# Opening pass of a transformer tower: three-part bf16 split by subtraction on TensorE, and another closing point for one of VectorE's loops

## The reference

```
h = W.T[x]                                        # embedding rows, (16, 512, 128)
x1 = layernorm(h)
left, right = x1 @ W1, W2 @ x1.T                  # W1 is 128x10, W2 is 10x128
h = h + softmax(left @ right / sqrt(512)) @ x1
x2 = layernorm(h)
h = h + ffn(x2)    # router picks 1 of 4 spatial and 1 of 4 temporal experts for each batch;
                   # three attentions of 8 heads (spatial S, temporal T and causal, cross C); an MLP
```

## Time and profile before

| | |
|---|---|
| three runs | 1670.5, 1671.6, 1672.09 us; median 1671.6 us |
| the profiled execution | 1672.9 us, span of its trace 1671.1 us |
| mean granted TensorE clock | 0.942 |
| TensorE, VectorE, ScalarE, GpSimd busy | 91%, 75%, 66%, 61% of the span |
| opening pass (start to `logits(0)`) | 0 to 134.8 us |
| second half of `embed_and_mix` | to about 250 us |
| `attend` | about 250 to 1555 us |
| `feed_forward` | to 1671.1 us |

### The profile page before, as it was taken

One profiled execution on the slowest core, in us unless ns is written; L12 is line 12 of the kernel. 1 busy time (PEld: TensorE's weight loads), 2 busy tenths in 40 slices (PEclk: granted clock), 3 DMA queues, 4 the chain that ended last, 5 costly groups with the idle time before them and its releaser, 6 DMA issues. The chain is left out here.

```text
span 1671.1 us, 37358 instructions
## 1 busy us (share of the span) xinstructions
PE 1517.6 (91%) x8662; PEld 661.0 (40%) x8662; DVE 1245.2 (75%) x3454; ACT 1106.5 (66%) x2137; POOL 1020.2 (61%) x1375
## 2 busy tenths in 40 slices
PE   3657976889999999999999999999999999875998
PEld 1215962233333333333333334333333333212665
DVE  6885866578887988888798888879788888353442
ACT  3333760647878788787877878787787878823333
POOL 6841435466686777767677777767767775523443
PEclk9867976889999999999999999999999999957999
DMA  1321118355554565456456546545655654121221
GB/s 48 77 52 30 45 32 110 49 77 74 75 84 66 72 78 83 64 77 82 64 75 78 79 63 80 79 63 79 78 76 62 86 70 50 15 25 33 64 63 57
DMA packets 134645, 109.27 MB, mean 65 GB/s; under 512 B 24128, under 2 KB 127552, under 8 KB 134592
## 3 DMA queue, kind: packets, MB, share of 16 engines
q1 hardware_dynamic: 132544, 104.45, 42.8%
q0 software_dynamic: 2048, 4.20, 1.0%
HBM read 19.26 MB, written 8.39 MB: 17 GB/s over the span
## 5 line engine op out<-in xcount | busy, mean ns | idle before, releaser
L1122 ACT ACTIVATE probs<-psum 128x512 f32<-128x512 f32 (+3 forms) x1536 | 755.7, 548 | 226.4 <-PE psum L1237 215.6
L1022 DVE TENSOR_REDUCE mx_S<-psum 128x1 f32<-128x512 f32 x512 | 326.3, 681 | 47.9 <-PE psum L1217 47.3
L1022 DVE TENSOR_REDUCE mx_C<-psum 128x1 f32<-128x512 f32 x512 | 318.0, 677 | 45.2 <-PE psum L1217 45.2
L1018 DVE CUSTOM_DVE_ANT_0 psum<-psum,causal 128x128 f32<-128x128 f32 (+3 forms) x512 | 243.3, 509 | 98.0 <-PE psum L1217 95.4
L1217 PE MATMUL psum<-ks_S,qs_S 96*128 96x512 bf16 x512 | 196.8, 395 | 10.8 <-DMA ks_S<-parts_k 6.1
L1217 PE MATMUL psum<-ks_C,qs_C 96*128 96x512 bf16 x512 | 199.7, 398 | 4.5 <-DMA ks_C<-parts_k 1.3
L1237 PE MATMUL psum<-qs_C,ks_C 99*128 99x512 bf16 x512 | 189.3, 385 | 3.6 <-ACT probs L1122 3.2
L1237 PE MATMUL psum<-qs_S,ks_S 99*128 99x512 bf16 x512 | 191.2, 385 | 0.2
L903 POOL CAST parts_q<-f_q 128x512 bf16<-128x512 f32 x48 | 29.3, 611 | 226.2 <-ACT f_q L1113 225.7
L1217 PE MATMUL psum<-ks_T,qs_T 96*128 96x128 bf16 (+3 forms) x512 | 156.1, 307 | 1.6 <-DVE mx_S L1022 1.0
L1237 PE MATMUL psum<-qs_T,ks_T 99*128 99x256 bf16 (+3 forms) x512 | 152.5, 302 | 2.8 <-ACT probs L1122 1.5
(11 more groups left out here) (182 smaller groups left out, 2720.2 us busy)
## 6 DMA issues: line engine op xcount, KB each, us to landing
qs_S<-parts_q SPq DMA_DIRECT2D x96, 128.0 KB, 4.4
ks_S<-parts_k SPq DMA_DIRECT2D x96, 128.0 KB, 4.8
qs_T<-parts_q SPq DMA_DIRECT2D x96, 128.0 KB, 4.4
ks_T<-parts_k SPq DMA_DIRECT2D x96, 128.0 KB, 4.6
qs_C<-parts_q SPq DMA_DIRECT2D x96, 128.0 KB, 4.3
ks_C<-parts_k SPq DMA_DIRECT2D x96, 128.0 KB, 5.0
w_in_S<-in_s_in SPq DMA_DIRECT2D x16, 257.0 KB, 2.8
w_in_T<-in_t_in SPq DMA_DIRECT2D x16, 257.0 KB, 2.7
```

The lines of the kernel that those rows point to most:

```text
L1018: nc.vector.tensor_tensor_reduce(tile[:, 0:last_key], tile[:, 0:last_key], causal[:, T - last_key:T], 1.0, NEG, ALU.add, ALU.max, mx[kind] ...
L1022: nc.vector.tensor_reduce(mx[kind][:, n:n + 1], tile, AX_X, ALU.max, negate=True).then_inc(reduced, 1)
L1122: nc.scalar.activation(probs[:, group_place(kind, b, n // 4), n % 4, t0:T], psum[:, LOGITS + ring_place(kind, b, n, RC), t0:T], ACT.Exp, s ...
```

## The change

Two things are changed.

**The opening pass.** `w12` is now 128 columns wide: the left weights stand six times beside each other (columns 10g to 10g+9), the right weights six times from column 64. One projection (fp32, 128 rows out) so gives the six copies of each factor at once, already stacked in PSUM. The remainders are then formed in the same PSUM bank: ScalarE casts the bank to bf16 (`part[0]`), TensorE adds `minus[:, 0] @ part[0]` to it (`take`), where `minus` is -1 on the diagonal of those groups that want a later part and 0 elsewhere; ScalarE casts again (`part[1]`), TensorE takes that away from the groups that want the third part. What is left in each group, rounded to bf16, is its part: ScalarE copies rows 0 to 63 to `qsd`, VectorE rows 64 to 127 to `ksd`. The score matmuls contract over 64 rows instead of 96. Gone are VectorE's subtraction, GpSimd's low part and the 12 stacking DMAs for a pair. The projection bank is doubled (banks 5 and 7).

ScalarE now normalises (four activations with scale and bias; VectorE makes `shift` = -mean * rstd), and SyncE copies `xs` to `X` by one DMA for each batch. Scores follow three batches late. GpSimd's gathers wait for the load of the ids alone. `logits(0)` waits for the last reduction instead of for `neg_step >= 6`; that wait is now ahead of `mix(0)`.

**VectorE's loop in `attend`** closes at slot 2, step 8: ahead of the ninth cross score.

```
-DVE_LOOP_AT = 1, 8
+DVE_LOOP_AT = 2, 8
...
-        MAXIMA, LR, TURN, POOLED = 4, 5, 6, 7
-        LO_LAG, SCORE_LAG, MAX_LAG = 4, 6, 7
+        MAXIMA, LR, TURN, POOLED = 4, (5, 7), 6, 7
+        TURN_LAG, PART_LAG, SCORE_LAG = 1, 2, 3
+        LATER = ((30, 60), (74, 94), (104, 114)), ((50, 60), (84, 94))
...
-                stack(0)
-                with sp.Fori(1, B // 2) as pair:
-                    stack(pair)
+                def keep(b, odd):
+                    sp.wait_ge(normed1, b + 1)
+                    sp.dma_start(X[:, bass.ds(NB * b, NB), 0:P], xs[:, odd, :, :]).then_inc(x_kept[odd], 16)
...
-                pool.wait_ge(loaded, 16 * LOADS)
+                pool.wait_ge(ids_in, 16)
...
-                for b in range(B + LO_LAG):
-                    if exists(b):
-                        fetch(b)
-                    if exists(b - LO_LAG):
-                        low_part(b - LO_LAG)
+                for b in range(B):
+                    fetch(b)
...
+                nc.vector.memset(minus[:], 0.0).then_inc(minus_set, 1)
                 dve.wait_ge(consts, 2)
+                dve.wait_ge(minus_set, 1)
+                for k, columns in enumerate(LATER):
+                    for a, e in columns:
+                        last = nc.vector.tensor_scalar(minus[:, k, a:e], ident[:, a:e], -1.0, None, ALU.mult)
+                last.then_inc(minus_set, 1)
+                nc.vector.memset(ksd[RA1:RA1 + 32, :, :], 1.0)
...
+                def take(c, odd, k):
+                    pe.wait_ge(part_ready[k], c + 1)
+                    nc.tensor.matmul(psum[:, LR[odd], :], minus[:, k, :], part[k][:], start=False, stop=(k == 1),
+                                     skip_group_check=True).then_inc(taken[k], 1)
...
-                pe.wait_ge(x_kept, B)
-                pe.wait_ge(neg_step, 6)
+                pe.wait_ge(x_kept[0], 8 * B)
+                pe.wait_ge(x_kept[1], 8 * B)
+                pe.wait_ge(reduced, 2 * B)
```

More of the change, by code:

```diff
@@ L269, in _ @@
                 sp.dma_start(norm_cols[:], norms).then_inc(loaded, 16)
[L271 to L280, removed]
-                stack(0)
-                with sp.Fori(1, B // 2) as pair:
-                    stack(pair)
+                def keep(b, odd):
+                    sp.wait_ge(normed1, b + 1)
+                    sp.dma_start(X[:, bass.ds(NB * b, NB), 0:P], xs[:, odd, :, :]).then_inc(x_kept[odd], 16)
+                halves_of_pairs(sp, keep, 1, B // 2, B // 2)
                 for half in range(2):
@@ new lines, in factors @@
+                    if exists(b):
+                        act.wait_ge(shift1, b + 1)
+                        at_least(act, turned1, b - 1)
+                        at_least(act, x_kept[odd], 16 * pair_of(b, odd))
+                        for n in range(NB):
+                            last = nc.scalar.activation(xs[:, odd, n, :], tokens(h, b, n), ACT.Identity,
+                                                        bias=shift[:, odd, n:n + 1], scale=rstd[:, odd, n:n + 1])
+                        last.then_inc(normed1, 1)
@@ L558, in turn_maxima, with scores @@
                         .then_inc(max_turned, 1)
+                def scores(c, half):
+                    at_least(pe, reduced, 2 * c - 1 + half)
+                    for n in range(2 * half, 2 * half + 2):
+                        last = nc.tensor.matmul(
+                            psum[:, n, :], qsd[0:RA1, bass.ds(c, 1), P * n:P * n + P].rearrange("p o t -> p (o t)"),
+                            ksd[0:RA1, bass.ds(c, 1), :].rearrange("p o t -> p (o t)"), start=True, stop=True)
+                    last.then_inc(scored, 1)
+                def take(c, odd, k):
+                    pe.wait_ge(part_ready[k], c + 1)
+                    nc.tensor.matmul(psum[:, LR[odd], :], minus[:, k, :], part[k][:], start=False, stop=(k == 1),
+                                     skip_group_check=True).then_inc(taken[k], 1)
                 def factors(b, odd):
@@ L585, in _ @@
-                halves_of_pairs(pe, factors, (SCORE_LAG + 1) // 2 + 1, B // 2, (B + SCORE_LAG + 1) // 2)
+                            last = nc.tensor.transpose(psum[:, TURN, P * n:P * n + P], xs[:, 1 - odd, n, :], ident[:])
+                        last.then_inc(turned1, 1)
+                    if exists(d):
+                        pe.wait_ge(q_ready, d + 1)
+                        pe.wait_ge(k_ready, d + 1)
+                        scores(d, 0)
+                    if exists(c):
+                        take(c, odd, 0)
@@ new lines, in factors @@
+                    if exists(t):
+                        pe.wait_ge(xT_ready, t + 1)
+                        at_least(pe, q_ready, t - 1)
+                        at_least(pe, k_ready, t - 1)
+                        nc.tensor.matmul(psum[:, LR[1 - odd], :], w12_t[:], xT[:], start=True, stop=False,
+                                         skip_group_check=True).then_inc(lr_ready, 1)
+                    if exists(c):
+                        take(c, odd, 1)
+                    if exists(d):
+                        scores(d, 1)
```

147 lines of the change are left out of this document (73 added, 74 removed).

## The result

| | kernel before | changed kernel |
|---|---|---|
| median (runs) | 1671.84 us (4) | 1644.07 us (4), 1643.43 to 1645.29 |
| ratio, 95% interval | | 0.9835, 0.982 to 0.9849 |
| profiled execution, span | 1672.9, 1671.1 us | 1643.73, 1642.0 us |
| first gather / start of the last | 5.52 / 96.70 us | 2.94 / 81.81 us |
| statistics of the last batch start | 101.32 us | 89.42 us |

I predicted 1641 us. In the profile 28.7 us are gained by `logits(0)`; the rest of the program takes as long as before (1216.4 us from the first to the last score of `attend`, before 1216.5).

A forecast was written before the change was run, and what follows sets the result against it. GpSimd and VectorE bound the opening pass, stacking its end, TensorE `attend`. Last statistics 84.7 + lateness 2.2 + tail 16.3 + low clock 0.8 put `logits(0)` at 104.0 us, 30.8 less: 1671.6 - 30.8 = 1640.8, thus 1641 us; range 1635 to 1653.

The forecast's parts named there:

- Start and pace of the gathers: Opening pass: GpSimd's first gather at about 2.8 us, later ones every 1.25 us, the last starting at 82.1 us.
- rival B: Opening pass: VectorE's memset of `ksd` keeps GpSimd out of SBUF, all gathers 7.7 us later, 1649 us; chance 0.05.
- Lateness behind the gathers: Opening pass: batches average 5.17 us with TensorE partly at low clock, 2.2 us late over 15 batches.
- Tail: End of the opening pass, from the last batch's statistics to `logits(0)`: 16.3 us, plus 0.8 us for low clock.
- Rival C: `attend`: VectorE's branch at the new point stops TensorE, 1659 us or up to 1683; chance 0.04, plus 0.03 for slower.
- `logits(0)`: Start of the second half, after the opening pass: predicted at 104.0 us against 134.80, 30.8 us less.
- I take 0: `attend`: VectorE's branch at slot 2, step 8 costs 0; a stop up to 1.15 us disappears in its wait.
- Range and chance of slower: Whole kernel: 1635 to 1653 us; faster 0.96, same 0.01, slower 0.03.
- keep up: Opening pass, per batch against 5.02 us: VectorE 4.6 us, ScalarE 4.05 us; TensorE follows at high clock only.

## Why the prediction was right, and where it was wrong

- **Start and pace of the gathers.** Right: first at 2.94 us (2.8), last at 81.81 (82.1), 0.94 to 0.95 us each, also beside VectorE's memset, so rival B did not happen. The "DVE blocks DMA" trap (the Trainium skill, SBUF — State Buffer) is about two-port operations of VectorE, and nothing here shows that this memset is one: it was no ground for rival B, and the trace says nothing against the rule.
- **Lateness behind the gathers, 2.2 us.** The term that was mis-sized: 5.0 us. The last gather was issued at 82.75, the last statistics started 6.7 us later, and 1.65 of that is the landing. All of it is pace. Up to batch 3 VectorE follows the gathers (24.50 us, where the landing was due at 24.50), and the twelve batches from there to the last take 64.92 us, 5.41 each against the gathers' 5.02, which is 4.7 us. Five of the twelve take 6.07 to 7.06 us and not the 5.91 that I had summed for TensorE alone, since waits between the engines come on top. The start costs nothing in the end: I weighed the memset only against GpSimd, and it holds VectorE itself, so that the first statistics begin at 11.24 and not at 9.4, but batch 1 starts at 14.49 and has caught up. VectorE in the changed kernel:

```profile
4.01 6.88 DVE L368 MEMSET ksd<- 32x8192 bf16 x1 [1.76 <-issue]
...
11.24 0.29 DVE L346 BATCH_NORM_STATS2 six<-h 128x6 f32<-128x128 f32 x1
```

- **Tail.** 106.11 - 89.42 = 16.7 us, predicted 16.3 + 0.8 = 17.1. Right.
- **A reading that was wrong.** GpSimd's last gather before was over at 96.70 + 0.94 = 97.64 us; at 99.93 a low part ended. So 37.2 us lay behind the last gather and not 34.9. The sum doesn't use this. Rival C took the 1.75 us before VectorE's first memset for the fetching of code; the trace before has no 8 KB packet of instructions from 0 to 25.6 us, so it doesn't show that.
- **`logits(0)`.** 28.7 us earlier, predicted 30.8; the 2.1 us missing are 2.8 us more lateness, less 0.4 of the tail and 0.3 of the gathers.
- **Closing point, "I take 0".** The number held only by luck, and its reason failed. I priced the branch at its new place by the wait that covers it, and found it hidden; the measured change between (1, 8) and (2, 8) is nothing with the old pass. But the same edit undoes a cost that the first part of the change brings in, and I had no term for that: removing 90 instructions ahead of a hardware loop moves the loop. Rival C had the mechanism (fetching code behind a branch) and the wrong place for it: it looked at the new closing point, and the danger was the old one. Its upper case of 3.5 us for each closing (1683 us) is near what the old point costs with the new pass: VectorE stops for 3.6 us, a period grows by 3.2, and the kernel takes 1680.41; in the cross slot it is 0.9. That VectorE's loop came to lie well in the changed kernel was not planned in the prediction.
- **Range and chance of slower.** The comparison fell inside. On chip 10 the kernel is slower by 27.6 us, which no rival foresaw, and four profiles of padded kernels on chip 6 lose the same 60 us in the opening pass. That ScalarE, VectorE and TensorE "keep up" with gathers without a pause was true of their work, and there untrue of their semaphores.

## What to carry to other kernels

When a change removes or adds instructions ahead of a hardware loop, look at where the loop's code comes to lie: count the instruction packets in the middle of the loop, and if they are there move the loop by padding or by another closing point before judging the change. Time a change on more than one chip when it takes the last pauses out of an engine that issues DMAs: with a pause of 1.18 us for each batch this one was still 21.9 us faster on chip 6 (one run), where the same pass without it, in kernels with 90 padding instructions, lost 26 to 29 us. And where TensorE stands between its clock levels, less work on it can cost time and idle matmuls can give some back.

## What was not expected of the hardware

- A branch back costs VectorE 0.3 us or about 4 us (635.31 to its next instruction at 639.42) for the same loop of 313 instructions, by its place alone; a period of 73.4 us grows by 2.5 and 4.0 us in turn, 3.2 in the mean.
- While GpSimd issued a gather every 1.25 us without a pause, the other engines' semaphores came up to 14 us late in every profile of chips 6 and 10. One was VectorE's to itself. On chip 15, and in the first comparison, nothing of it is to be seen at the same pace.
- Six bf16 matmuls that nobody reads took the mean of a batch from 5.4 or 5.5 to 5.0 us on the same chip; a projection 1.4 us shorter took it to 5.73, with TensorE at the low level throughout.
